# Cross-attention and quantised feed-forward on one core: VectorE's queue is written in another order around the row sums

## The reference, cut to what matters

```python
x = x + xattn(layernorm(x), ctx)          # 16 heads of 64, context of 64 rows per batch
#   q = LN(lat) @ Wq ; k, v = LN(ctx) @ Wkv
#   attn = softmax(clip(q k^T / 8, -11, 11)) ; out = attn v @ Wo + bo
x = x + ffn(layernorm(x))                 # 8-bit fake quantisation of x, weights and hidden
#   xq = quant(x), one scale for the whole tensor: sigmoid(clip) * max|x| / 127
#   h = quant(silu(xq @ Wg^T) * (xq @ Wu^T)) ; out = h @ Wd^T
```

## Time and profile before

| what | us |
|---|---|
| median of three runs (lowest, highest) | 1312.22 (1311.52, 1313.82) |
| the profiled execution, its own time | 1311.13 |
| its span, first to last instruction | 1309.2 |
| PE busy, share of the span | 1263.4, 96% |
| DVE busy | 1093.7, 84% |
| ACT busy | 800.9, 61% |
| POOL busy | 277.1, 21% |
| mean granted TensorE clock | 0.996 |

### The profile page before, as it was taken

How to read it: one execution, slowest core, us unless ns; L and a number is a source line. 1 busy time by engine, 2 the same in 40 slices (tenths; PEclk the granted TensorE clock), 3 DMA queues, 4 the chain that set the end, 5 groups by cost and what they waited for, 6 DMA issues and landing times.

```text
span 1309.2 us, 20493 instructions
## 1 busy us (share of the span) xinstructions
PE 1263.4 (96%) x7607; PEld 583.7 (45%) x7607; DVE 1093.7 (84%) x2117; ACT 800.9 (61%) x1211; POOL 277.1 (21%) x227
## 2 busy tenths in 40 slices
PE   6999899999999999999999999999999999999998
PEld 4644444444444444444444443444444444434443
DVE  7777878878877877887787768799999999889998
ACT  6688576567558657756765772233333333399993
POOL 2105231441342144034224330000000000013233
PEclk9999899999999999999999999999999999999999
DMA  8276156248156264452553392196667542389997
GB/s 297 81 234 185 35 144 203 79 108 222 57 140 191 77 179 133 118 197 73 153 197 91 99 245 106 41 307 211 219 257 264 203 170 85 113 313 417 419 418 304
DMA packets 182436, 241.74 MB, mean 185 GB/s; under 512 B 122032, under 2 KB 141248, under 8 KB 169920
## 3 DMA queue, kind: packets, MB, share of 16 engines
q1 hardware_dynamic: 182336, 240.43, 55.8%
HBM read 120.86 MB, written 90.57 MB: 161 GB/s over the span
## 4 chain that ended last, share of the span: by engine, by line
PE 33%; DVE 27%; ACT 16%; POOL 9%; issue 8%; DMA 7%; SPq 1%; POOLq 0%; ACTq 0%; DVEq 0%
PE pg L1575 11%; PE pu L1581 11%; POOL esum L396 8%; ACT hb L1439 4%; ACT E L453 3%; DVE E L668 3%; DVE p L672 3%; ACT E L459 3%; DVE st L608 3%; ACT E L463 2%; PE po L77 2%; PE po L79 2%; PE po L78 2%; DVE st L682 2%; DVE x L679 2%
## 5 line engine op out<-in xcount | busy, mean ns | idle before, releaser
L1417 ACT ACTIVATE sg<-pg,gate_scale 128x512 f32<-128x512 f32 x176 | 120.9, 687 | 183.5 <-PE pg L1575 183.5
L77 PE MATMUL po<-VW,p 128*128 128x512 f16 x480 | 183.4, 382 | 14.0 <-DVE x_rows L679 10.4
L77 PE MATMUL ring<-yT,M 128*128 128x512 f16 x512 | 194.4, 380 | 0.0
L79 PE MATMUL ring<-yT,M 128*128 128x512 f16 x512 | 194.3, 380 | 0.0
L78 PE MATMUL ring<-yT,M 128*128 128x512 f16 x512 | 194.3, 380 | 0.0
L79 PE MATMUL po<-VW,p 128*128 128x512 f16 x480 | 183.2, 382 | 0.0
L78 PE MATMUL po<-VW,p 128*128 128x512 f16 x480 | 183.0, 381 | 0.0
L1575 PE MATMUL pg<-xqT,w 128*128 128x512 bf16 x704 | 180.7, 379 | 1.0 <-ACT xqT L1428 0.8
L1581 PE MATMUL pu<-xqT,w 128*128 128x512 bf16 x704 | 180.7, 380 | 0.0
L474 ACT ACTIVATE p<-E 128x512 f16<-128x512 f32 x120 | 74.7, 623 | 164.1 <-DVE E L668 164.0
L1491 DVE TENSOR_TENSOR hb<-pu,sg 128x512 f32<-128x512 f32 x176 | 120.8, 687 | 26.5 <-PE pu L1581 25.0
(11 more groups left out here) (238 smaller groups left out, 2017.9 us busy)
## 6 DMA issues: line engine op xcount, KB each, us to landing
hidden<-hb SPq DMA_DIRECT2D x11, 2816.0 KB, 9.7
xa<-x_rows_d SPq DMA_DIRECT2D x28, 1024.0 KB, 5.8
hb<-hidden SPq DMA_DIRECT2D x22, 1024.0 KB, 16.2
x<-in_x_dram SPq DMA_DIRECT2D x16, 1024.0 KB, 6.4
value_fold<-E SPq DMA_DIRECT2D x64, 256.0 KB, 2.5
VW<-value_fold SPq DMA_DIRECT2D x16, 1024.0 KB, 6.6
x_rows_d<-x SPq DMA_DIRECT2D x16, 1024.0 KB, 4.1
out_dram<-xa SPq DMA_DIRECT2D x11, 1024.0 KB, 12.9
```

Source lines behind the costliest of these rows:

```text
L77: nc.tensor.matmul(out, a_hi, b_hi, start=first, stop=False)
L79: return nc.tensor.matmul(out, a_lo, b_hi, start=False, stop=last)
L1417: nc.scalar.activation(sg[:, n % 4], pg[n % 4][:], ACT.Silu, scale=gate_scale[:, n % FT:n % FT + 1]).then_inc(silus, 1)
```

## The change

Five things are written differently, all in the attention part. No arithmetic changes, and the count of instructions on each engine stays.

1. GpSimd: the sums of step s wait for all low probability halves of group s-1 (`prob_lo`), in steps 1 to 14. Before it was steps 2 to 14, and they also waited for all low row halves of group s+1 (`y_lo`). In step 0 the bias comes behind the sums and not between them.
2. VectorE in steps 2 to 14: `take(s-1, 0)` stands ahead of `low_y(s+1, 3)`; `unit_range` moves behind the first four folds; `invert` moves behind `take(s-1, 1)` and the last four folds.
3. Group 2's statistics and rows leave step 0 and move to step 1, on VectorE and ScalarE: `high_y(2, 0..3)` stand behind the last `exp` of step 1.
4. In step 1 the probabilities of group 0 are divided one beside each score part, where before parts 0 to 7 stood beside score parts 2 to 7.
5. In step 15 and behind it `invert(15)` stands ahead of `take(14, 0)`, `take(14, 2)` is split in two, `take(14, 3)` stands behind all divisions, and `take(15, 0)`, `take(15, 1)` and the last rounding stand around `centre`.

```diff
     def highs_beside(s, t):
         if s == 1:
-            return ((), (), (0,), (1,), (2, 3), (4,), (5,), (6, 7))[t]
+            return (t,)
         return (t + 2,) if s > 1 and t < 6 else ()
     def row_beside(s, t):
-        if s + 1 == NG:
-            return None
-        return {5: 2, 7: 3}.get(t) if s == 1 else {3: 0, 4: 1, 6: 2, 7: 3}.get(t)
+        return {3: 0, 4: 1, 6: 2, 7: 3}.get(t) if 1 < s and s + 1 < NG else None
-    LOW_BESIDE = ((), (), (), (), (0,), (1,), (), (2, 3))
+    LOW_BESIDE = ((), (), (), (), (0,), (1,), (), (2,))
...
-            if s > 1 and more:
+            if s > 0 and more:
                 pool.wait_ge(prob_lo, 8 * s)
-                pool.wait_ge(y_lo, 4 * (s + 1) + TT)
             for t in range(1, KT):
                 add_up(s, t)
-                if s == 0 and t >= 4:
-                    bias(s + 1, t - 4)
-            if s > 0 and more:
+            if more:
                 for t in range(TT):
                     bias(s + 1, t)
...
-                if s == 1 and t == 1:
-                    high_y(2, 0)
-                    high_y(2, 1)
...
+            if s == 1:
+                for t in range(TT):
+                    high_y(2, t)
...
-        def take(g, t):
+        def take_sum(g, t):
...
+        def take_stats(g, t):
...
+        def take(g, t):
+            take_sum(g, t)
+            take_stats(g, t)
...
-                    if t == 4:
-                        norm_stats(2)
+                    continue
+                if s == 1:
+                    if t in (2, 3):
+                        norm_stats(2, (2 * t - 4, 2 * t - 3))
                     if t == 5:
                         norm_aggregates(2)
-                    if t == 6:
                         norm_rstd(2, 2)
-                    continue
-                if s == 1:
-                    if t in (4, 6):
-                        norm_rows(s + 1, t // 2)
-                    if t in (5, 7):
-                        low_y(s + 1, t // 2)
+                    if t == 7:
+                        norm_rows(2, 0)
+                        norm_rows(2, 1)
                     continue
...
-                norm_rows(2, 0)
-                norm_rows(2, 1)
                 invert(0)
-                low_y(2, 0)
-                low_y(2, 1)
                 continue
+            if not more:
+                continue
+            if s == 1:
+                for t in range(2):
+                    low_y(2, t)
+                    norm_rows(2, t + 2)
+                low_y(2, 2)
+            take(s - 1, 0)
+            low_y(s + 1, 3)
+            for u in FOLD_AFTER[0]:
+                fold(s, u)
             if s <= UNITS:
                 unit_range(s - 1)
-            take(s - 1, 0)
-            if more:
-                for u in FOLD_AFTER[0]:
-                    fold(s, u)
+            take(s - 1, 1)
+            for u in FOLD_AFTER[1]:
+                fold(s, u)
             invert(s)
-            if more:
-                take(s - 1, 1)
-                for u in FOLD_AFTER[1]:
-                    fold(s, u)
-                round_unit(s - 1)
...
+            round_unit(s - 1)
+            take(s - 1, 2)
+            divide(s, 0)
+            take(s - 1, 3)
+            divide(s, 1)
+            low(s, 0)
         last = NG - 1
+        unit_range(last - 1)
+        invert(last)
+        take(last - 1, 0)
+        for t in range(3):
+            divide(last, t)
+        low(last, 0)
         take(last - 1, 1)
-        divide(last, 0)
-        divide(last, 1)
-        low(last, 0)
-        round_unit(last - 1)
-        take(last - 1, 2)
-        for t in range(2, KT):
+        low(last, 1)
+        for t in range(3, 5):
             divide(last, t)
             low(last, t - 1)
-            if t == 5:
-                take(last - 1, 3)
+        take_sum(last - 1, 2)
+        for t in range(5, KT):
+            divide(last, t)
+            low(last, t - 1)
         low(last, KT - 1)
+        take_stats(last - 1, 2)
+        take(last - 1, 3)
         keep.range_of_rows(dve, 0, TT * last)
+        take(last, 0)
         keep.centre(dve)
-        for t in range(TT):
+        take(last, 1)
+        round_unit(last - 1)
+        for t in range(2, TT):
             take(last, t)
```

More of the change, by code:

```diff
@@ L680, in take @@
                                            ALU.add, ALU.max, row[:, 2:3]).then_inc(outs_taken, 1)
+        def take_stats(g, t):
+            xt, row = x[:, g % 4, t], keep.rows[:, TT * g + t]
             dve.wait_ge(outs_taken, 4 * g + t + 1)
@@ L981, in on_vector @@
-        last = NG - 1
-        take(last - 1, 1)
-        divide(last, 0)
-        divide(last, 1)
-        low(last, 0)
-        round_unit(last - 1)
-        take(last - 1, 2)
-        for t in range(2, KT):
+            round_unit(s - 1)
+            take(s - 1, 2)
+            for u in FOLD_AFTER[2]:
+                fold(s, u)
+            divide(s, 0)
+            take(s - 1, 3)
+            divide(s, 1)
+            low(s, 0)
+        last = NG - 1
+        unit_range(last - 1)
+        invert(last)
```

## The result

| | before | after |
|---|---|---|
| median, us (lowest, highest) | 1312.95 (1311.52, 1313.82) | 1291.81 (1291.67, 1291.84) |
| ratio, 95% interval | | 0.984 (0.9823 to 0.9857) |
| span of the profiled execution | 1309.2 | 1290.0 |

A forecast was written before the change was run, and what follows sets the result against it. It took a loop of waits among PE, DVE and POOL as the bound in steps 3 to 14. 17.8 + 4.2 - 2.7 = 19.3 us off 1311.13 gives 1291.8, plus 1.09 for the median: 1293.0, range 1288.5 to 1299.

The forecast's parts named there:

- 1.1 added for the median: Whole kernel: the median of runs lies 1.09 us above the profiled execution, so 1291.8 becomes 1292.9, stated as 1293.0.
- Steps 3 to 14: Steady attention steps: PE's waits go, value steps gain 1.73 us and key steps 1.2, together 17.8 (16.7 to 18.6).
- the drain: Key and value steps: each PE wait also hides some 0.1 us of drained array that counts as busy.
- Step 15: Group 15's scores to the last matmul: waits for low halves and half clock go, gain 4.2 us (2.5 to 4.4).
- the half clock: Behind step 15's waits: 3.55 us at granted clock 0.57, costing about 1.7 us, part of the gain there.
- The narrowest place: Behind step 15: take(15, 0)'s sum ends at 51.6 us, PE wants it at 51.8; a miss costs some tenths.
- Steps 0 and 1: Start of attention: a long PE wait before the third key fold, half clock behind it; 2.7 us lost (0 to 4.5).
- The holding in the steady steps: Steady steps: POOL's sums hold two low_y a step, 2.5 us on DVE, within its idle time; nothing reaches PE.
- A: Rival on steps 0 and 1: the start costs nothing, 22.0 us gained, 1290 us; chance 0.15.
- B: Rival on the steady steps: one per-step wait partly stays, returning 0.5 us in 12 steps, 1299 us; chance 0.14.
- C: Rival: POOL's sums hold every DVE operation, so the second take is late and the kernel slower, 1366 us; chance 0.03.
- D: Rival: the change doesn't remove the wait, PE's bound is something step 2 hides; within 0.2% of before; chance 0.03.

The follow-up runs named there:

- the version that has it: Changed kernel with group 2's rows prepared beside step 1's score parts, its statistics in step 0, and two more exps before group 0's first high half: 1282.2 us.
- 1311.25 with the loop back: Changed kernel; in steps 2 to 14 GpSimd waits for all low row halves and VectorE has the old order, invert before the second take: 1311.25 us, ratio 1.000.

## Why the prediction was right, and where it wasn't

The time was forecast within 1.2 us, and the mechanism of the steady steps was right. That the sum came out so close is in part luck. The steps gained 1.6 us more than forecast and the start lost 1.7 more, and these cancel: 19.3 forecast, 19.2 to 19.3 between the profiles. The 1.2 us are the 1.1 added for the median, which this kernel didn't show (profile 1291.84, median 1291.81), and a rounding.

- **Steps 3 to 14.** 17.8 forecast, 19.4 measured, above the 18.6 of my bound. A key step gained 1.38 and not 1.2, since I had the drain too small. The rows of PE in step 7 of the kernel before show all of it: two waits of 0.80 and 0.22 us idle, but 429.18 - 428.00 = 1.18 from start to start where 0.22 is usual, and two runs of 48 fold matmuls 1.09 apart where the run itself takes about 0.7. Some 0.96 and 0.40 are lost, so each wait costs 0.16 to 0.18 us more than its idle time.

```profile
421.12 0.87 PE L1044 MATMUL ring<-kvb,w 64*128 64x64 f16 x48
422.21 0.87 PE L1044 MATMUL ring<-kvb,w 64*128 64x64 f16 x48 [0.22 <-DVE M L637]
428.00 0.38 PE L79 MATMUL po<-VW,p 128*128 128x512 f16 x1
429.18 0.39 PE L77 MATMUL po<-VW,p 128*128 128x512 f16 x1 [0.80 <-DVE x_rows L679]
```

  A value step gained 1.80, since step 2 itself fell from 44.56 to 44.49. Taking step 2 as the price of a step without waits was right, but the reason given, "its POOL had no `y_lo` stall to pass on", was wrong: POOL waited 39.8 us in it, and DVE 3.8 for POOL. What it lacked was a late step ahead of it. The waits went as said. What the prediction didn't say is that the loop had two links, and that opening either would have done; part 1 of the change is surplus beside part 2, and the other way round.
- **Step 15.** 4.2 forecast, 4.2 measured. Of these the half clock, for which I had 1.7, isn't tied to the order: with the old order and the loop open the same waits come without it, and the order is worth 3.0. The narrowest place held as well: `take(15, 0)`'s sum ends before PE wants its bank, with no wait in the rows.
- **Steps 0 and 1: the term that was mis-sized.** 2.7 lost was forecast, "between 0 and 4.5"; 4.4 were. The place was right: one long wait ahead of the third key fold, with half clock behind it. The step that failed is "If POOL's sums, which start at 135.2 in this step, hold the low halves, it is 1.2 more", of which I then took half. The rows show all four `low_y` held, 3.4 us over 0.69 each (1.07 + 1.06 + 1.06 + 0.22), and the four `norm_rows` too, 2.6 over the 0.54 or so of each (0.96 for two, 0.82, 0.83), which I had not thought of at all. ACT's second pair of high halves waits behind these. With the sums out of the way the wait is 3.78, so the 4.4 forecast without holding were enough and the holding was worth 2.55 us, not 0.6. The half clock lasted 5.7 us and not 3.5, and took 2.7 us and not 1.7 to 2: 1.2 on the fold matmuls (2.71 us where 1.51 is usual) and 1.5 on seven that start each 0.43. 2.55 and some 1.1 of half clock make the 3.7 between the two starts of step 2. This second part can't be put down to the change: in two of the five kernels with these very steps and this very wait the half clock is as short as without the holding. And of the two waits at group 0's outputs there is only one, 1.51, where I had 2.0 in two.
- **The holding in the steady steps.** "Two `low_y` a step of over 1 us" is wrong in its detail. In step 7, which two of VectorE's instructions are held shows in these rows of the changed kernel:

```profile
409.54 0.93 DVE L628 TENSOR_TENSOR y<-y 128x512 f16<-128x512 f32 x1 [2.16 <-ACT y L419]
...
414.58 0.66 DVE L628 TENSOR_TENSOR y<-y 128x512 f16<-128x512 f32 x1
415.16 2.72 DVE L632 SCALAR_TENSOR_TENSOR M<-ring,key_cols,M 128x512 f16<-128x512 f32 x4
417.80 1.21 DVE L699 TENSOR_REDUCE row_scale<-ffn_raw 128x2 f32<-128x1024 f32 x1
419.04 1.23 DVE L701 TENSOR_SCALAR row_scale<-row_scale 128x2 f32<-128x2 f32 x1
...
425.05 0.70 DVE L649 STREAM_TRANSPOSE esum_by_token<-esum 128x512 f32<-128x512 f32 x1
```

  One `low_y` takes 0.93, the other none extra; a product of 2 x 128 numbers takes 1.23, on average 1006 ns where it was 258. That one stands beside GpSimd's addition of the bias (417.73 to 422.71), not beside the sums. The folds beside the sums are at 0.68 each. `invert` follows without idle time, where VectorE stood idle for 3.78 in step 6. Nothing of it reached PE, as said.
- **The rivals.** A's free start didn't come; the version that has it takes another arrangement (1282.2). B's remaining wait didn't come. C is refuted by the folds and takes at their old durations. D is refuted by the steps at 44.5 and 44.7 us, and 1311.25 with the loop back shows that it was the loop that had kept them longer.

The Trainium skill (SBUF — State Buffer, "Who interferes with whom") has more on the holding than I used. I had written that an instruction with a single SBUF input doesn't contend; the page says so only of one outside the two-port modes, and a `tensor_scalar` that runs in such a mode takes the shared ports for a whole instruction. The trace agrees with this and not with my shortening: `norm_rows`, with one tensor in SBUF, takes 1.37 beside a sum and 0.55 without. In which mode it ran, the trace doesn't show.

One thing stays open: why the half clock behind the same wait is long in one profile and shorter or missing in another.

## What to carry to other kernels

When A waits for B, B for C and C for A's last step, every lateness read from the trace belongs to the loop and goes with it: don't carry such a start time into the walk of a changed order. Before rewriting an engine's order, try each link alone, since one line out of one queue gave all that the rewrite of the steps gave. A pipeline's first and last rounds need an account of their own: here the last gave and the first took 3 to 4 us, and the first had 10 us in it for whoever arranged it apart.

## What the hardware did that I had not expected

- GpSimd's fp32 sum also holds `tensor_scalar` with one tensor in SBUF: 0.55 to 1.37 us. A small one can pay as much as a large one: 128x2 numbers rise from 0.27 to 1.23 beside the bias. It needn't: the same instruction takes 0.17 where it starts between two sums, as in the kernel before without GpSimd's wait.
- The holding seems to go both ways: in step 7 GpSimd's first sum took 1.50 where it took 1.27 before, and the next six took 9.12 where they took 8.3 (415.94 to 425.68 in all before).
- How long PE stays at the lower of its two clock levels (1.2 of 2.4 GHz) doesn't follow from the length of the wait. Behind 6.3 us it stayed there for 5.7 us in the changed kernel (2.7 us lost) and for 3.3 to 5.7 in the four others with the same wait; behind 4.0 us (no wait for the probabilities) for 5.5. Behind 1.9 us in step 15 it was 3.5 us at 0.57 in the kernel before, and nothing, 1.00, in two others.
